# A megakernel of four layers: DVE's order in the delta loop, and banks and order in the drain behind it

## What is computed

```python
def step(carry, inp):
    fH, sH, ns = carry
    k_t, v_t, q_t, i_t, nu_t, p_t = inp
    pred = (einsum(q_t, fH) + einsum(q_t, sH)) * 0.5
    err = sum((v_t - pred) ** 2); surprise = sigmoid(err / (TEMP + 1e-06))
    d_fast = kv - k_t * einsum(k_t, fH);  fH = fast_alpha * fH + (1 - fast_alpha) * d_fast
    d_slow = kv - k_t * einsum(k_t, sH);  sH = slow_alpha * sH + (1 - slow_alpha) * u_slow * d_slow
    ns = ns + u_neu * (nu_t - ns) * 0.1
    o = p_t[0] * einsum(q_t, fH) + p_t[1] * einsum(q_t, sH) + p_t[2] * ns
...
x = x + L0_attn(layernorm(x));  x = x + L0_ffn(layernorm(x))
x = x + L1_attn(layernorm(x));  x = x + L1_ffn(layernorm(x))
```

## Time and profile before

| | us |
|---|---|
| median of 3 runs | 2117.74 (2117.61 to 2119.97) |
| the profiled execution | 2109.22 |
| its span | 2107.5 |
| PE busy in the span | 1907.0 (90%) |
| DVE busy | 1357.6 (64%) |
| ACT busy | 963.3 (46%) |
| POOL busy | 247.8 (12%) |

### The profile page before, as it was taken

How to read it: one execution, slowest core, us unless ns; L and a number is a source line. 1 busy time by engine, 2 the same in 40 slices (tenths; PEclk the granted TensorE clock), 3 DMA queues, 4 the chain that set the end, 5 groups by cost and what they waited for, 6 DMA issues and landing times. The chain is left out here.

```text
span 2107.5 us, 31872 instructions
## 1 busy us (share of the span) xinstructions
PE 1907.0 (90%) x11154; PEld 1617.0 (77%) x11154; DVE 1357.6 (64%) x2810; ACT 963.3 (46%) x1801; POOL 247.8 (12%) x229
## 2 busy tenths in 40 slices
PE   8999999983999999996777589998999999999999
PEld 5788888872899999994445357776888888888887
DVE  7567788774666666665999878884444445345342
ACT  4656666643444444435888555542323232232221
POOL 0000012334233232331000000000000000000000
PEclk9999999995999999998888789999999999999999
DMA  3299411323544332233223413413000000000000
GB/s 105 72 364 408 149 49 59 113 84 106 144 106 88 81 85 47 41 46 110 70 60 90 97 44 120 160 51 139 1 21 20 0 20 9 11 20 0 20 11 11
DMA packets 86146, 170.32 MB, mean 81 GB/s; under 512 B 7264, under 2 KB 49888, under 8 KB 85856
## 3 DMA queue, kind: packets, MB, share of 16 engines
q1 hardware_dynamic: 65968, 132.47, 18.0%
q0 software_dynamic: 18176, 33.70, 8.1%
q10 hardware_dynamic: 1888, 2.67, 0.4%
HBM read 91.61 MB, written 88.74 MB: 86 GB/s over the span
## 5 line engine op out<-in xcount | busy, mean ns | idle before, releaser
L2690 ACT ACTIVATE x_tok<-bank,scl 128x512 f32<-128x512 f32 x128 | 88.3, 690 | 360.2 <-PE bank L2741 359.4
L2740 PE MATMUL bank<-hAh,ffn_h 128*128 128x512 f32 x512 | 202.7, 396 | 0.7 <-DVE x_tok L2617 0.7
L2740 PE MATMUL bank<-hBh,ffn_h 128*128 128x512 f32 x512 | 201.7, 394 | 0.0
L2741 PE MATMUL bank<-hAl,ffn_h 128*128 128x512 f32 x512 | 199.4, 389 | 0.0
L2741 PE MATMUL bank<-hBl,ffn_h 128*128 128x512 f32 x512 | 199.3, 389 | 0.0
L1487 POOL DMA_INDIRECT tokens_behind_spare_rows<-yg,row_of_token x70 | 129.5, 1850 | 302.7 <-DVE row_of_token L1655 283.1
L1590 ACT ACTIVATE h<-bank,b1s 128x256 f32<-128x256 f32 x280 | 124.8, 472 | 31.9 <-PE bank L1415 19.8
L2598 DVE CAST hBh<-x_tok 128x1024 fp32r<-128x1024 f32 x48 | 33.3, 693 | 157.6 <-ACT x_tok L2690 157.0
L2598 DVE CAST hAh<-x_tok 128x1024 fp32r<-128x1024 f32 x48 | 33.3, 693 | 148.7 <-ACT x_tok L2690 148.2
L911 ACT ACTIVATE L<-bank 128x512 f32<-128x512 f32 x128 | 75.4, 595 | 106.1 <-PE bank L1169 105.9
L1177 PE MATMUL bank<-st,L 128*128 128x128 f32 x768 | 116.3, 278 | 6.3 <-DVE st L549 6.2
(11 more groups left out here) (447 smaller groups left out, 5498.6 us busy)
## 6 DMA issues: line engine op xcount, KB each, us to landing
z_by_expert<-zero SPq DMA_DIRECT2D x64, 520.0 KB, 16.0
ckb<-in_ffn_dram POOLq DMA_DIRECT2D x32, 352.0 KB, 3.5
xg<-z_by_expert SPq DMA_DIRECT2D x36, 260.0 KB, 3.3
x_tok<-in_w_dram SPq DMA_DIRECT2D x8, 1024.0 KB, 7.7
ffn_h<-ffn_copy SPq DMA_DIRECT2D x2, 4096.0 KB, 14.9
x_tok<-after_time_mix SPq DMA_DIRECT2D x15, 512.0 KB, 7.5
st<-in_w_dram SPq DMA_DIRECT2D x6, 1024.0 KB, 7.3
x_tok<-x_T SPq DMA_DIRECT2D x9, 512.0 KB, 4.2
```

The source lines that it names most:

```text
L2690: A_.activation(gq[:, m % 4, :], B[2 + m % 4][:, :], ACT.Gelu, scale=scl[:, off[nm] + m:off[nm] + m + 1]).then_inc(g_act, 1)
L2740: T.matmul(out, w, x[0], start=first, stop=False)
L2741: return T.matmul(out, w, x[1], start=False, stop=last)
```

## The change

On DVE, in the loop: `new_state` is split into `next_state` (two operations) and `partial_outputs` (six). For chunk 0 the second part moves from ahead of apply(3) to behind it; for chunk 1 from ahead of apply(6) to behind apply(7). The scan `neurons` moves from behind `masks` and `residual` to ahead of `masks`. `variances` moves from the odd turn (lag 5, ahead of apply(1)) to the end of the even turn before it (lag 4, behind `stats`).

In the drain: the columns of block 6 get banks 7 and 6 in place of 7 and 7, and their second half waits until DVE has read the last partial results in bank 6 and no longer for ScalarE's first copy. DVE takes `stats`, `take_ranks`, `variances`, `mean_squares` and `norm` in another order and `gates(b5)`, `places(b5)` behind them; ScalarE puts `columns(b6, 0)`, `columns(b6, 1)` ahead of `norm_root(b7)` and `out_root(b7)` behind `norm_root(b6)`; TensorE puts `output(b6)` behind the second `predict`. No instruction is added or taken away.

```diff
@@ bank_of
-            return (bank_behind if b == LAST else bank_in_turns)[item]
+            return (7, 6) if (b, item) == (LAST - 1, "z") else (bank_behind if b == LAST else bank_in_turns)[item]
@@ DVE
-            def new_state(t, j):
+            def next_state(t, j):
                 ...
                 last.then_inc(f_rdy, 1)
+            def partial_outputs(t, j):
+                c = t * 2 + j
                 ...
                 dve.wait_ge(f_rdy, c + 2)
+
+            def new_state(t, j):
+                next_state(t, j)
+                partial_outputs(t, j)
@@ DVE turn(u)
                 at(u, 1, 7, gates)
                 at(u, 1, 7, take_ranks)
-                at(u, 1, 5, variances)
                 ...
                 if tail:
-                    new_state(t - 1, 0)
+                    next_state(t - 1, 0)
                 if deltas:
                     apply(t, p, 3)
+                if tail:
+                    partial_outputs(t - 1, 0)
+                at(u, 1, 3, neurons)
                 if head:
                     masks(t + 1, 1 - p, 0)
                 at(u, 0, 4, residual, 0)
-                at(u, 1, 3, neurons)
                 at(u, 1, 7, places)
                 ...
                 if tail:
-                    new_state(t - 1, 1)
+                    next_state(t - 1, 1)
                 if deltas:
                     apply(t, p, 6)
                 ...
                 if deltas:
                     apply(t, p, 7)
+                if tail:
+                    partial_outputs(t - 1, 1)
+                if deltas:
                     dve.wait_ge(ap_rdy, (t + 1) * (2 * LEVELS))
                     fold_words(t, 1)
                 at(u, 0, 2, neuron_gates)
                 at(u, 0, 4, stats)
+                at(u, 0, 4, variances)
                 at(u, 1, 3, mean_squares)
@@ DVE drain
             neurons(b7)
+            stats(b6)
+            outputs(b7)
+            take_ranks(b5)
+            variances(b6)
+            mean_squares(b7)
+            norm(b6)
             gates(b5)
-            take_ranks(b5)
             places(b5)
-            outputs(b7)
-            stats(b6)
-            mean_squares(b7)
-            variances(b6)
             out_scale(b7)
-            norm(b6)
             ...
+            gates(b7)
             take_ranks(b7)
-            gates(b7)
@@ ACT drain
             o_squares(b7)
-            out_root(b7)
             out_columns(b7)
             norm_root(b6)
+            out_root(b7)
             for h in range(2):
                 rows(b6, h)
-            norm_root(b7)
             columns(b6, 0)
             columns(b6, 1)
+            norm_root(b7)
@@ PE z1_columns
-                if k == 1 and b < LAST:
+                if k == 1 and b == LAST - 1:
+                    pe.wait_ge(pp_rdy, NC + 1)
+                elif k == 1 and b < LAST:
                     pe.wait_ge(z1T_rdy, 2 * b + 1)
@@ PE drain
             predict(t, t % 2, 0)
-            output(b6)
             y_state(t, 1)
             predict(t, t % 2, 1)
+            output(b6)
```

## The result

| | before | changed |
|---|---|---|
| median | 2117.68 us (4 runs, 2117.54 to 2119.97) | 2135.42 us (4 runs, 2132.89 to 2135.58) |
| profiled execution | 2109.22 us | 2135.58 us |
| span | 2107.5 us | 2133.9 us |
| ratio of the medians | | 1.0078 (95%: 1.0061 to 1.0096) |

The change is slower, as forecast, but by 17.7 us and not by 8.2; 2135.4 lies above the range of 2117 to 2132. The lines of the changed kernel are shifted: L1148 is now L1159, L1177 is L1188, L1220 is L1231, L1185 (the transposes of Y) is L1196, L1516 is L1529, and on DVE L601 is L607.

The account below looks back on a forecast made before the run. It took TensorE's idle time to bound the loop and GpSimd's last 16 stores the drain. Loop +11.8 and drain -3.6 gave +8.2 us: 2117.4 profiled, 2125.9 as median, range 2117 to 2132.

Parts of the forecast that it names:

- What bounds: Whole kernel: TensorE is busy 90% of the span, so a microsecond counts only where TensorE stands still.
- Chunk 0 behind apply(3), scan ahead of the masks: Loop: later masks make TensorE wait; +8.9 in odd turns, +7.0 in even ones, +2.1 in turns 1 and 2.
- Chunk 1 behind apply(7) and the boundary: Loop: removing the partial_sums wait gains 8.1 and 2.3; later apply(0) at even-to-odd boundaries costs 4.2.
- the terms -0.46 and +0.37: Odd turns 5 to 13: 0.46 gained at apply(6) each; five even-to-odd boundaries: net 0.37 lost each.
- 5 x 0.75 = 3.75: Even-to-odd boundaries: early variances free ScalarE, removing TensorE's 0.61 wait for the squares, 0.75 with refill.
- Loop: Delta loop: all loop terms together +11.8 us, bounds +7.6 to +14.
- The clock: Loop: TensorE's granted clock was to stay at 1.00 despite new 2.1 us waits, so nothing was added.
- rival C: Loop: the clock falls in six odd turns, +14 on top of 8.2, so 2140 us; chance 0.07.
- Drain: Loop end to first expert: new column bank and orders start block 6's stores earlier; -3.6 us, bounds -2.0 and -4.8.
- Turn 15: Last loop turn: the 1.1 gain at apply(6) meets a scan 1.05 later, priced at 0.
- From the profiled execution to the median: Whole kernel: the 8.5 us by which the median exceeded the profiled execution was carried over, 2117.4 to 2125.9.

Follow-up runs that it names:

- e2: Changed kernel with the scan back behind masks and residual, chunk 0's partial outputs still behind apply(3): 2123.19 us, ratio 1.0021.
- e3: Changed kernel with the scan and chunk 0's partial outputs both back in their old places: 2106.67 us, ratio 0.9938.
- e1: Changed kernel with 16 unread identity transposes filling TensorE's wait for the masks in odd turns 3 to 15: 2124.53 us, ratio 1.0027.
- e7: Kernel before with only chunk 0's partial outputs moved behind apply(3), scan left behind the masks: 2127.30 us, ratio 1.0092.
- e5: Kernel before, unchanged, profiled once more: 2109.01 us, ratio 1.0004.
- e8: Kernel before with chunk 1's partial outputs behind apply(7) and the variances behind stats, nothing else: 2100.94 us, ratio 0.9968.
- e6: Kernel before with only chunk 1's partial outputs moved behind apply(7): 2105.08 us, ratio 0.9987.
- e13: Kernel before with four unread constant reductions on DVE ahead of the masks in odd turns from 3 on: 2136.13 us, ratio 1.0099.
- e14: Kernel before with three unread constant reductions on DVE ahead of the masks in odd turns from 3 on: 2131.68 us, ratio 1.0077.
- e9: Changed kernel, run again without further edits: 2134.98 us, ratio 1.0076 to the kernel before.
- e15: Repeat of the changed kernel with scan and chunk 0's partial outputs back in their old places, new drain kept: 2101.80 us, ratio 0.9938.
- e16: Repeat of the kernel before with chunk 1's partial outputs behind apply(7) and early variances, old drain: 2105.45 us, ratio 0.9958.
- e10: Changed kernel with the drain of the kernel before, so the loop's edits alone: 2136.18 us, ratio 1.0083.
- e4: Kernel before with only the drain of the changed kernel: 2116.30 us, ratio 0.9990.
- e12: Kernel before with only the scan moved ahead of the masks in odd turns: 2120.82 us, ratio 1.0008.
- e11: Repeat of the changed kernel with scan and chunk 0's partial outputs back in their old places, new drain kept: 2105.38 us, ratio 0.9942.

## Why the prediction was wrong, point by point

**What bounds.** Right as far as the waits go: TensorE's new waits are for the masks. But not all of the new time stands in waits, as the text had it; some of it stands in matmuls at half clock.

**Chunk 0 behind apply(3), scan ahead of the masks: +18.0 (8.9 + 7.0 + 2.1).** Right. The wait is 2.07 for 2.1 in the odd turn; in the even one it is 0.75 at the transposes and 0.70 at level 5, of which the earlier trace rows had 0.48, about 1.0 of idling for the 1.17. Measured without the clock, from turn 1 to 14: 15.4 for chunk 0 (e2 less e3) and 2.0 for the scan (e1 less e2), 17.4; turn 1 itself adds 1.1 (21.48 in e7, 20.37 in e5), 18.5. The wait for nsT is gone as said. The split inside was off: chunk 0 costs 1.16 in odd turns too (e7), and the scan less than the 1.30 less 0.62 allowed for.

**Chunk 1 behind apply(7) and the boundary: -10.4 + 4.2 = -6.2.** Right in sign, 2.4 to 2.6 too small in size. From turn 1 to 14 e8 shows -7.8 and e3 -7.6, and turn 1 itself gives another 1.0. The waits for partial_sums and for ScalarE are gone. At the boundary the new wait for st is 0.33 (the row at 412.37), not 1.1, but most of the forecast delay is there: that row starts 6.76 behind the last level of turn 12 (5.84 before, 6.96 forecast), and TensorE loses the rest in shorter waits ahead of it. Turn by turn, an even one gives 1.0 and not 0.90, and an odd one with its boundary 0.3 to 0.4 (turns 7 to 13, 23.33 in e8 where before has 23.65 to 23.74) where the terms -0.46 and +0.37 gave 0.09. The variances alone are worth 3.6 (e8 less e6), and the text had 5 x 0.75 = 3.75.

**Loop: +11.8.** Without the clock 313.7 - 303.9 = 9.8 (e1), inside 7.6 to 14. So far the sum held, 2.0 high.

**The clock: 0 in the sum, rival C at 0.07.** This is the step that failed. The prediction put it so: "between these waits TensorE works without a gap for 10 us or more, and a single wait of 2.1 is shorter than 3.28". Both halves are true and neither protects. With 10 us of unbroken work behind it the clock fell after 2.07 (changed kernel), after 1.96 and 0.68 (e13) and after 1.37 and 0.68 (e14). The only wait that I had beside a fall was the 3.28 of turn 0, and the longest harmless one was 1.0 (with the clock at 1.00 in the earlier trace rows); 2.1 lay between, where I had no row, and I priced it at nothing. C's time, 2140, was also too high, because I priced a fall at 2.3 us from turn 0, and it costs about 1.6: 8.2 over the five turns in which it fell in the first profile, 9.4 in e9 where it fell in six. The Trainium skill, "TensorE: Matmul & The Clock Gate", section "What's actually happening", has the default throttled and activity releasing it. The traces agree in so far as the clock fell behind idling and held where that was filled (e1). They also show how little idling it took: here it fell in a stretch where TensorE was busy 259.46 of 281 us.

**Drain: -3.6, bounds -2.0 and -4.8.** Right in sign, at the low bound in size. Pairs with and without these edits differ by 2.7 (e15, e16) and 2.2 (e9, e10) between turn 15 and the first expert. e4 against the two profiles of before gives 2.8 and 3.0, but there 1.4 is the longer row of stores (20.5 from the first to the last for 19.1, one long store in each of the two), which e12 and e16 with the drain of before don't have; that part isn't the change's. The stores of block 6 begin 2.5 (e15 less e16, measured from turn 15) and 2.0 (e9, e10) earlier, not 3.6. The column's waits of the earlier trace rows are gone, as said: the eight transposes stand in one row with 0.53 ahead of them. The logits even come 4.8 earlier (e15 less e16); what is given back is DVE's wait for ScalarE's exponentials, 2.64 for 0.17, a step that the sum didn't have.

**Turn 15: 0.** Open in part. By the two profiles it is 8.7, but they are from different surroundings. Inside one job the changed kernel (28.5) has 1.5 more than e12, whose turn 15 is nearly that of before (27.0); e10, with the changed kernel's loop, has none (27.0). The 1.5 between e9 and e10 goes with the clock: in e9 one stop makes TensorE wait 2.22 and the clock reads 0.50 behind it, in e10 it is spread over 0.80 and 0.55 and the clock stays at 1.00. So 0 to 1.5 is all that the change can have there, the rest is the surroundings.

**From the profiled execution to the median: 8.5 carried over.** I gave no reason for it, and it came out by luck: medians of before of 2108 and 2118 occur, 10 us apart, and the first profile (2109.22) is of the first kind while its timed runs are of the second. The changed kernel's profile (2135.58) has no such distance from its median (2135.42).

Together: 9.8, 8.2 to 9.4 for the clock, 0 to 1.5 for turn 15, less 2.2 to 2.8 in the drain, is 15 to 18.5, and the medians differ by 17.7 and 16.6 (e9's job). Of the 9.5 by which the forecast was low the clock alone makes 8.2 to 9.4; that the loop came 2.0 below its forecast stands against it, and the drain's missing 0.9 to 1.4 and turn 15 roughly make that up.

## What to carry to other kernels

Before work is put ahead of a producer, read how much slack its consumer has, and the consumers of what stands behind it in the queue: here it was 0.4 us at the masks and none at the scan and apply(4) behind them, so six operations of 1.17 us cost 1.16 in every turn. Work of 1.2 us fits in a stretch where the next thing in line is not waited for, and then a wait really goes (chunk 1 behind apply(7)); the two halves of one edit had opposite signs. When an edit leaves TensorE one wait that is longer than any in the profile of a steady loop, price the clock too: a fall costs its own time on top (about 1.6 us here), it is not excluded by TensorE being busy 92% of the stretch, and filling the gap with matmuls that nobody reads gets it back.

## What the runs showed of the hardware

- In the odd turns 3 to 13 of a busy loop the granted clock fell in 17 of 18 cases after one wait of 2.00 to 2.07 (the changed kernel twice, and e10), in six of six after 1.96 and then 0.68 (e13), in five of six after 1.37 and then 0.62 to 0.69 (e14), and in none after 0.75 and then 0.62 to 0.69 (e2, e7, 12 cases) or after 0.84 to 0.90 alone (e12, six cases). With the same wait of 2.00 it fell in one execution of a program and not in another. Each fall cost about 1.6 us.
- The length of a wait doesn't settle it. In turn 15 of e2 the clock fell to 0.50 behind waits of 0.73 and 0.91, and in e11 it stayed at 1.00 behind 0.66 and 0.91.
- Sixteen transposes in the gap, which left 0.30 idle, kept it at full speed and made the kernel 8.2 us faster from turn 1 to 14 (e1).
- The same kernel took 2107.98, 2114.47, 2118.32 and 2118.41 us in four jobs. Half or more of the difference stands in one stretch, the last turn before the drain, in waits that nothing in the trace releases (20 to 23 us where before took 2108, 26 to 29 where it took 2118). Two profiles of one program from different jobs differ there by nearly 5 us (e3 28.8, e15 24.0).
